# A graph attention kernel: the weighted sums are taken at the end of a step's first half, the copies of V are issued by ScalarE, and GpSimd takes the reciprocals of the row sums

## The reference

```python
q, k, v = (proj(Wq, bq), proj(Wk, bk), proj(Wv, bv))
scores = jnp.einsum('bhqd,bhkd->bhqk', q, k) * SCALE
mask = (adj_matrix + bond_matrix)[:, None, :, :]      # both are adj
attn = jax.nn.softmax(scores * mask, axis=-1)
ctx = jnp.einsum('bhqk,bhkd->bhqd', attn, v)
out = jnp.einsum('bse,fe->bsf', ctx, Wo) + bo
x = _layernorm(x + out, axis=-1)
```

## Time and profile before

| | |
|---|---|
| median of 3 runs | 419.25 us (416.65 to 419.89) |
| profiled execution | 418.86 us, span 416.3 us |
| TensorE's mean granted clock | 0.989 |
| PE busy | 382.1 us, 92% |
| DVE busy | 386.2 us, 93% |
| ACT busy | 361.6 us, 87% |
| POOL busy | 249.6 us, 60% |
| DMA engines, share over most slices | 0.8 to 0.9 |

### The profile page before, as it was taken

One profiled execution on the slowest core, in us unless ns is written; L12 is line 12 of the kernel. 1 busy time (PEld: TensorE's weight loads), 2 busy tenths in 40 slices (PEclk: granted clock), 3 DMA queues, 4 the chain that ended last, 5 costly groups with the idle time before them and its releaser, 6 DMA issues.

```text
span 416.3 us, 12182 instructions
## 1 busy us (share of the span) xinstructions
PE 382.1 (92%) x3628; PEld 291.4 (70%) x3628; DVE 386.2 (93%) x1592; ACT 361.6 (87%) x1223; POOL 249.6 (60%) x379
## 2 busy tenths in 40 slices
PE   8989999999996999999999999899999999997772
PEld 6766777777674877777777776677777777675542
DVE  4988999999997799999999999999999999999865
ACT  4699999989897798999999999889899999999560
POOL 3143557677573775748577575757758474555455
PEclk9999999999999899999999999999999999999898
DMA  8468889989988789889989888888999898888632
GB/s 272 131 173 238 236 201 254 245 237 247 244 237 234 191 223 244 244 243 251 253 237 246 241 237 235 230 242 233 248 245 248 227 232 208 219 234 183 144 105 76
DMA packets 65427, 92.29 MB, mean 222 GB/s; under 512 B 8529, under 2 KB 48722, under 8 KB 65362
## 3 DMA queue, kind: packets, MB, share of 16 engines
q1 hardware_dynamic: 47426, 66.35, 63.9%
q10 hardware_dynamic: 17936, 25.17, 18.0%
HBM read 26.22 MB, written 8.39 MB: 83 GB/s over the span
## 4 chain that ended last, share of the span: by engine, by line
DVE 33%; PE 28%; DMA 12%; SPq 11%; issue 9%; ACT 4%; POOL 1%; DVEq 0%; ACTq 0%; POOLq 0%
DVE boxes L540 15%; DVE probs L521 13%; SPq L208 9%; DMA v_boxed<-v 8%; PE ctx_bank L404 7%; PE out_bank L421 5%; PE proj_bank L333 5%; PE out_bank L351 4%; PE row_bank L264 3%; ACT probs L728 3%; DMA carried<-boxes 3%; PE turn_bank L281 2%; SPq L217 2%; DVE stats L567 1%; DVE low_top L530 1%
## 5 line engine op out<-in xcount | busy, mean ns | idle before, releaser
L728 ACT ACTIVATE probs<-probs,low_top 128x256 f32<-128x256 f32 x512 | 254.6, 504 | 12.1 <-DVE low_top L530 12.1
L521 DVE CUSTOM_DVE_ANT_0 probs<-row_bank,adj_rows 128x256 f32<-128x256 f32 x512 | 187.4, 414 | 6.7 <-PE row_bank L264 5.9
L540 DVE STREAM_TRANSPOSE boxes<-probs 128x1536 f32<-128x1536 f32 x62 | 109.6, 1768 | 0.0
L333 PE MATMUL proj_bank<-xt_parts,w_parts 128*128 128x512 f32 x360 | 99.2, 411 | 0.0
L728 ACT ACTIVATION_READ_ACCUMULATOR probs<-probs,low_top 128x1 f32 x512 | 99.1, 194 | 0.0
L333 PEld LDWEIGHTS proj_bank<-xt_parts,w_parts 128*128 128x128 f32 x360 | 62.9, 188 | 30.5 <-issue 19.9
L404 PE MATMUL ctx_bank<-carried,v_boxed 128*32 128x256 f32 x744 | 61.9, 392 | 18.3 <-DMA v_boxed<-v 12.2
L867 POOL COPY wide<-shares 128x512 f32<-128x512 f32 x32 | 19.5, 610 | 92.2 <-DVE shares L548 92.2
L264 PE MATMUL row_bank<-kq 32*128 32x256 f32 x1024 | 73.3, 400 | 0.5 <-DVE top L521 0.5
L404 PEld LDWEIGHTS ctx_bank<-carried,v_boxed 128*32 128x32 f32 x744 | 32.3, 111 | 43.4 <-issue 31.4
L264 PEld LDWEIGHTS row_bank<-kq 32*128 32x128 f32 x1024 | 46.3, 184 | 11.7 <-issue 6.4
(11 more groups left out here) (85 smaller groups left out, 461.1 us busy)
## 6 DMA issues: line engine op xcount, KB each, us to landing
carried<-boxes SPq DMA_DIRECT2D x248, 192.0 KB, 3.9
xt<-in_x_t SPq DMA_DIRECT2D x32, 256.0 KB, 3.5
adj_rows<-in_adj ACTq DMA_DIRECT2D x32, 256.0 KB, 4.8
xr<-in_x ACTq DMA_DIRECT2D x32, 256.0 KB, 3.8
v_boxed<-v SPq DMA_DIRECT2D x124, 64.0 KB, 3.0
out<-result ACTq DMA_DIRECT2D x31, 256.0 KB, 5.3
w_whole<-in_wk ACTq DMA_DIRECT2D x2, 128.0 KB, 3.7
w_whole<-in_wq SPq DMA_DIRECT2D x1, 256.0 KB, 4.3
```

Of the source, the lines that this page charges most:

```text
L333: last = nc.tensor.matmul(proj_bank[:], w_parts[:, a, which, t, c * P:(c + 1) * P], xt_parts[:, pair % 2, b, t, :], start=(half_ == 0 and ...
L521: last = nc.vector.tensor_tensor_reduce(probs[:, h % RING, t * S:(t + 1) * S], row_bank[j][:, t * S:(t + 1) * S], adj_rows[:, (g // 2) % 2 ...
L540: nc.vector.transpose(boxes[:, n % BOXES].rearrange("p a h (f q) -> p (h f) a q", q=D), probs[:, first:first + BOXED, :].rearrange("p h (f ...
L728: last = nc.scalar.activation(tile, tile, ACT.Exp, bias=low_top[:, g % 2, J * c + j, t:t + 1], accum_out=sums[:, g % 2, t, j * T + c:j * T ...
```

## The change

- `weigh_v(g - 2)` moves behind the output projection and `turn_shares(g - 2)` in the first half of step g. The inverses of graph g-2 are now turned in that half, and no longer in the second half of the step before; `project_out` moves from the second half of step g (graph g-2) to its first half (graph g-3); `project_v(g + 1)` moves to the second half.
- DVE follows: `add_residual(g - 3)`, box, `aggregate(g - 4)`, then `scale_context(g - 2)` last in the first half. One step more lies between a graph's sums and its result.
- `lower_tops` lowers two heads at once: two reductions of four elements per group in place of four of two.
- `divide` moves to POOL, as a power of -1 over 16 elements; the last graph's stays on DVE.
- `carry_v` moves from SP's queue to ACT's, at slot 6 (behind `copy_v` at slot 5), with four semaphores in place of two. `copy_inverse(g - 2)` moves ahead of slot 0, `load_masks` to slot 4.
- The end of the program is ordered anew: `project_out` of graph 29 and the sums of graph 30 now stand between the transposes of the last graph, and POOL scales and normalises graph 28 ahead of `spread_shares` of the last one.

The diff, without the declarations of `minus_ones`, its semaphore and `v_in`, and without the end of DVE's, ACT's and POOL's programs where the list above tells it:

```diff
@@ -209,15 +212,6 @@
                                  ).then_inc(carried_in[n % 4], 16)
-            def carry_v(n):
-                sp.wait_ge(v_ready, n + 1)
-                wait(sp, ctx_made, n - 3)
-                for j in range(J):
-                    sp.dma_start(v_boxed[j::J, (n // 2) % 2, n % 2].rearrange("p t e -> p (t e)"),
-                                 v[D * j:D * (j + 1), (n // 2) % 2, n % 2].rearrange("p t e -> p (t e)")
-                                 ).then_inc(v_in[n % 2], 16)
@@ -275,7 +266,7 @@
                 wait(pe, moved, n)
-                wait(pe, inverted, n // 2)
+                wait(pe, inverted, (n + 1) // 2 - 1)
@@ -360,7 +351,7 @@
                 else:
-                    pe.wait_ge(moved, 2 * g + 2)
+                    pe.wait_ge(moved, min(2 * g + 3, 2 * LAST))
                 for half_ in range(2):
...
                         last = nc.tensor.transpose(turn_bank[:, half_ * S + t * P:half_ * S + (t + 1) * P],
@@ -371,7 +362,7 @@
             def weigh_v(g):
...
                 if g < LAST:
-                    pe.wait_ge(v_in[g % 2], 64 * (g // 2 + 1))
+                    pe.wait_ge(v_in[g % 4], 64 * (g // 4 + 1))
@@ -468,37 +459,38 @@
                 ahead = g // 2 + 1
-                if g < B:
-                    rows(2 * g)
+                rows(2 * g)
                 if is_pair(ahead):
...
                     make_bias()
+                if is_graph(g - 3):
+                    project_out(g - 3)
                 if is_graph(g - 2):
+                    turn_shares(g - 2)
                     weigh_v(g - 2)
-                if is_group(2 * g - 1):
-                    turn_probs(2 * g - 1)
-                if is_graph(g + 1):
-                    project_v(g + 1)
-                if is_graph(g):
-                    rows(2 * g + 1)
+                turn_probs(2 * g - 1)
+                rows(2 * g + 1)
                 if is_pair(ahead):
...
                         project_kq(ahead, 2 * (g % 2) + 1, half_)
-                if is_graph(g - 1):
-                    turn_shares(g - 1)
-                if 0 <= g - 2 < LAST:
-                    project_out(g - 2)
-                if 0 <= g < LAST:
+                if is_graph(g + 1):
+                    project_v(g + 1)
+                if g < LAST:
                     turn_probs(2 * g)
...
                 step(g)
-            for c in range(T):
-                for j in range(J):
-                    turn_last(c, j)
+            turn_shares(LAST - 1)
+            for j in range(3):
+                turn_last(0, j)
+            project_out(LAST - 2)
+            for c, j in ((0, 3), (1, 0), (1, 1)):
+                turn_last(c, j)
             weigh_v(LAST - 1)
+            for j in (2, 3):
+                turn_last(1, j)
@@ -524,11 +516,12 @@
                 last.then_inc(rows_used, 1)
-            def lower_top(n, j):
-                g, place = n // T, J * (n % T) + j
-                dve.wait_ge(rows_used, J * n + j + 1)
-                nc.vector.tensor_reduce(low_top[:, g % 2, place, :], top[:, g % 2, place, :].unsqueeze(2), AXIS.X, ALU.max,
-                                        negate=True).then_inc(top_ready, 1)
+            def lower_tops(n, half_):
+                g, place = n // T, J * (n % T) + 2 * half_
+                dve.wait_ge(rows_used, J * n + 2 * half_ + 2)
+                nc.vector.tensor_reduce(low_top[:, g % 2, place:place + 2, :], top[:, g % 2, place:place + 2, :].unsqueeze(3),
+                                        AXIS.X, ALU.max, negate=True).then_inc(top_ready, 2)
@@ -541,11 +534,11 @@
                                     ).then_inc(boxed, 1)
-            def divide(g):
-                dve.wait_ge(probs_ready, H * g + H)
-                wait(dve, widened, g)
-                nc.vector.reciprocal(shares[:], sums[:, g % 2]).then_inc(shares_ready, 1)
...
@@ -655,11 +648,9 @@
                     reduce_rows(n, j)
-                    if j > 0:
-                        lower_top(n, j - 1)
-                    if j == 1 and n % T == 0 and n > 0:
-                        divide(n // T - 1)
-                lower_top(n, J - 1)
+                    if j == 2:
+                        lower_tops(n, 0)
+                lower_tops(n, 1)
             def step(g):
                 if is_group(2 * g):
@@ -669,29 +660,35 @@
                 if g == 1:
...
                     nc.vector.tensor_copy(bias[:], ctx_bank[:, 0:E]).then_inc(bias_ready, 1)
-                if 0 <= g - 2 < LAST:
-                    scale_context(g - 2)
+                if is_graph(g - 3):
+                    add_residual(g - 3)
                 if is_group(2 * g - 1):
                     box(2 * g - 1)
-                if 0 <= g - 3 < LAST:
-                    aggregate(g - 3)
-                if is_group(2 * g + 1):
-                    mask_group(2 * g + 1)
-                if 0 <= g - 2 < LAST:
-                    add_residual(g - 2)
-                if 0 <= g < LAST:
+                if is_graph(g - 4):
+                    aggregate(g - 4)
+                if is_graph(g - 2):
+                    scale_context(g - 2)
+                mask_group(2 * g + 1)
+                if g < LAST:
                     box(2 * g)
-                if 0 <= g - 2 < LAST:
+                if is_graph(g - 3):
                     for t in range(T):
-                        row_stats(g - 2, t)
+                        row_stats(g - 3, t)
             for g in range(B):
                 step(g)
-            for c, j in ((0, 2), (0, 3), (1, 0), (1, 1), (1, 2)):
-                move_last(c, j)
-            divide(LAST)
+            aggregate(LAST - 3)
+            for j in (2, 3):
+                move_last(0, j)
+            add_residual(LAST - 2)
+            for j in (0, 1):
+                move_last(1, j)
+            for t in range(T):
+                row_stats(LAST - 2, t)
+            scale_context(LAST - 1)
+            divide_last()
+            move_last(1, 2)
             aggregate(LAST - 2)
-            scale_context(LAST - 1)
@@ -723,6 +720,9 @@
                 act.wait_ge(top_ready, J * n + j + 1)
+                if c == 0 and j == 0:
+                    wait(act, shares_ready, g - 1)
@@ -773,6 +773,15 @@
                                out_bank[:]).then_inc(v_ready, 1)
+            def carry_v(n):
+                act.wait_ge(v_ready, n + 1)
+                wait(act, ctx_made, n - 3)
+                for j in range(J):
+                    act.dma_start(v_boxed[j::J, (n // 2) % 2, n % 2].rearrange("p t e -> p (t e)"),
+                                 v[D * j:D * (j + 1), (n // 2) % 2, n % 2].rearrange("p t e -> p (t e)")
+                                 ).then_inc(v_in[n % 4], 16)
@@ -809,26 +818,32 @@
                     n, j = 2 * g + s // J, s % J
+                    if s == 0 and is_graph(g - 2):
+                        copy_inverse(g - 2)
                     if is_group(n):
                         exp(n, j)
-                    if s == 0 and 0 <= g - 4 < LAST:
-                        store(g - 4)
+                    if s == 0 and is_graph(g - 5):
+                        store(g - 5)
                     if s == 0 and g == 0:
...
                         copy_v(0)
-                    if s == 2 and is_graph(g + 2):
+                    if s == 2 and g == 0:
+                        carry_v(0)
+                    if s == 6 and 0 <= g + 1 < LAST:
+                        carry_v(g + 1)
+                    if s == (4 if g > 0 else 2) and is_graph(g + 2):
                         load_masks(g + 2)
...
                         move_turned(2 * g - 1)
+                    if s == 5 and is_graph(g + 1):
+                        copy_v(g + 1)
                     if s == 6 and is_graph(g):
                         load_x(g)
-                    if s == (3 if g > 0 else 5) and is_graph(g + 1):
-                        copy_v(g + 1)
                     if s == (3 if g > 0 else 4) and is_pair(ahead):
                         read_kq(ahead, 2 * (g % 2) + 1)
-                    if s == 3 and is_graph(g - 1):
-                        copy_inverse(g - 1)
+                    if s == 2 and g == LAST:
+                        copy_inverse(LAST - 1)
@@ -859,6 +874,15 @@
                 nc.gpsimd.tensor_tensor(low, xt[:, pair % 2, t, :], high.bitcast(F32), ALU.subtract).then_inc(xt_low, 1)
+            def divide(g):
+                pool.wait_ge(probs_ready, H * g + H)
+                wait(pool, widened, g)
+                if g == 0:
+                    pool.wait_ge(minus_ones_ready, 1)
+                nc.gpsimd.tensor_tensor(shares[:].rearrange("p t h -> p (t h)"), sums[:, g % 2].rearrange("p t h -> p (t h)"),
+                                        minus_ones[:], ALU.pow).then_inc(shares_ready, 1)
@@ -922,23 +947,26 @@
                 for s in range(H):
-                    if s == 0 and is_graph(g - 1):
+                    if s == 0 and g % 2 == 1 and is_pair(g // 2 + 2):
```

(42 more changed lines are left out.)

## The result

The changed kernel takes 512.32 us (median of 6 runs, 509.81 to 517.67), the kernel before 416.7 in the same runs: 1.227 times as long, 95% interval 1.2205 to 1.2337. I forecast 432, slower, with 439 as the upper end. The direction and the place of the loss were right, its size was not: 95.6 us where I gave about 13.

A forecast was written before the change was run, and what follows sets the result against it. ACT, idle 1.5 us a step behind V's issues, was to bound the kernel at 12.55 us against 12.08: 29 steps give +13.6, then +2.5, -0.6 and -2, +13.5 on 418.86, or 432 us; range 403 to 439.

The forecast's parts named there:

- What bounds the kernel: Kernel before: PE's work bounds a step at about 11.5 us; the mean step is 12.08, leaving 0.58 to win.
- the sums' move: On PE, sums behind output projection and turned inverses: 1.85 us covers most waits for boxes, bringing PE near 11.5 us.
- Rival 1: V's issues on ACT hidden, PE bounds: step 11.5 to 11.6 us, 401.5 us (398 to 413); chance 0.30.
- DVE: Fewer, wider reductions and no reciprocal: 0.4 to 0.8 us less a step, about 11.1 us, no bound.
- ACT takes V's copies: Five issues on ACT's queue take 2.85 to 3.1 us against 1.45 of cover: 1.5 us idle, step 12.55 us.
- POOL: Power over 16 elements on POOL: 0.7 to 4.3 us, 2.5 taken; up to 4.0 hidden under a 12.55 us step.
- Rival 3: POOL bounds: a power of 4.3 us makes a step of 12.8 us, 438 to 446 us; chance 0.08.
- The end: Last step: PE's 2.78 us wait for boxes goes, but POOL's 2.7 us for a graph precedes the shares; net -2.

## Why the prediction was wrong

- **What bounds the kernel, the sums' move.** Right. PE's waits for DMA ahead of the sums went from 18.2 to 1.0 us (0.9 with V on SP, 7.0 with the order alone), and without ACT's stall the order wins 2.9% (406.8 us). Rival 1's 401.5 us is met by the kernel with spread issues (402.6), whose steps are bounded by PE as it said: 149.40 us busy of 150. Its condition did not come, an issue of V at 0.33 us; the issues are hidden because they stand apart.
- **DVE.** The forecast was 13 to 25 us less busy time; from before to the profile after it is 5.3 us (386.2 to 380.9), and in the kernel with V on SP 12.1 (374.1). It was costed as no bound, and is none: with the reductions single again the time stayed (405.7 against 405.6).
- **ACT takes V's copies: the term that was mis-sized.** Forecast: issues of 2.85 to 3.1 us, a lead of 1.45, a stall of 1.5. Measured: in two steps of the middle 4.85 and 5.32 us of issues (203.98 to 208.83 and 218.93 to 224.25), a lead of 1.45 and 1.46 (to 205.43 and 220.39), and a stall of 3.6 in the mean. The mean step, from the first power at 29.71 to the 31st at 478.93, is 14.97 us, not 12.55. The failed step is the sentence that left out SP's dear issues as "a sign of a crowded queue, which ACT's x load never shows". ACT's x load was a single issue, and a single one was cheap even beside a busy neighbour: before the change it stood at 167.27, inside SP's four issues of V (the row below), and took 0.33 us. In the changed kernel, too, the first of the five takes 0.48 to 0.53 us in every step; the later ones, beside SP's boxes, take up to 1.58. No row that the prediction took from ACT's queue had several issues on end, so it could not tell the price of a row. With the collision taken away the issues are 612 to 616 ns and the row is 3.05 us (221.90 to 224.95), as forecast.

```profile
166.36 2.95 SPq L217 DMA_DIRECT2D v_boxed<-v  x4
```

- **What I did not see: the wait sets the moment.** I counted the wait for V as 0.85 us of lead lost. Taken away, it is worth 103 us (512.3 less 409.0); put back with other data, it costs them again. The traces show how the two queues meet (times of one step of the changed kernel). ACT's stall ends at 208.88 and its copy of the inverses comes at 210.45; PE's transpose in the middle of the step waits for that until 211.16 (83.6 us of such waits in all); behind it come the scores of the second half, DVE's mask and its box (216.16 to 217.94), and SP's box copies from 217.97, which then fall on ACT's next issues of V from 218.93. That this loop holds itself is my reading of the order of events; shown are its ends, by SP's added wait (57 us less) and by the wait's removal and return. With SP's added wait the mean step is 12.98 us (powers at 29.7 and 419.0), and at best 12.77 to 12.79: ACT's 11.05 of work and a stall of 1.73, where I had forecast 11.05 and 1.5. In nearly half of the steps the stall there is longer, up to 2.87, and why was not taken apart. So the forecast would have been some 23 us too low even then (454.8 against 432).
- **POOL.** The power takes 2.91 us, inside 0.7 to 4.3 and 0.4 above the value taken. Rival 3 did not come. With V on SP POOL is busy 139.19 of 150 us in the middle, so the power leaves it little room there.
- **The end.** Forecast -2 us net. In the changed kernel 19.9 us lie between the last exponential (489.69 + 0.19) and the end, against 16.0 before. POOL reaches the last shares 4.6 us behind that exponential (494.45), against 1.1 before, and PE waits up to 2.4 us for them. That this is the cause is not shown: in the run with POOL's end reordered the wait shrank and the time did not. The granted clock over this end is lower too, 0.83 against 0.93.
- **The Trainium skill's sentence** ("DMA: Bandwidth & Descriptors", section "Issuing engines are not separate DMA queues"), that the sequencer's time is usually small beside the transfer, would have led to rival 1. Taken singly the trace of the changed kernel agrees: the median issue of V is 0.91 us, against 3.9 from issue to landing. Spread out or without the wait the time is near rival 1's too (402.6 and 409.0 us); in a row behind a wait on ACT's own result the same issues cost 110 us (512.3 less 402.6).

## What to carry to other kernels

In this kernel a DMA issue on ACT's queue was free as long as it took less time than the work already handed out. So count how much work stands between the last wait and the issues, and put issues one at a time behind different pieces of work. A semaphore wait ahead of them does more than cut that lead: it ties the moment of the issues to the engine's own progress, and so to whatever else starts at that moment. When a price is taken from another place, ask two things: whether it was a single issue or one of a row, and what the other queue was doing at the time. Single issues stayed cheap here nearly always (with V's issues spread out the median is 496 ns, beside a few of up to 1992), and rows on both queues at once did not.

## What the runs showed of the hardware

- Issues of ACT are slower when they stand in a row while SP issues its box copies. With SP's queue quiet V's issues took 0.48 to 0.63 us; in the steps shown of the changed kernel, beside SP's boxes, the first took 0.49 or 0.50 and the later ones 0.9 to 1.44. x's load took 334 ns alone, 0.59 behind V's row with SP quiet, and mostly 0.8 to 1.6 there beside SP's boxes.
- Single issues of ACT kept their price beside a busy SP queue: 0.33 us for x's load before the change, and 496 ns in the median for V's issues spread out.
- POOL's power took 708 ns for 2 elements of a partition and 2914 for 16, by which I estimate some 158 ns for each element more.
- Behind a wait of 2.95 us TensorE's granted clock was 0.63 over 4.5 us (212.80 to 217.30), and six matmuls of K and Q took 2.93 us instead of 1.66.
